# A new order of the attention step, queries turned in pairs, and a first expert choice over eight batches

## The reference, cut to what matters

```
x = x + tanh(g_xattn[0]) * conv_mix(layernorm(x), k, bias, ctx, ctx)        # stage A
x = x + tanh(g_ffn[0])   * moe(layernorm(x))        # stage B: shared FFN + top 2 of 8 experts
x = x + tanh(g_xattn[1]) * mha(layernorm(x), ctx, ctx)  # stage C: 16 heads, causal
x = x + tanh(g_ffn[1])   * lora_moe(layernorm(x))   # stage D: one FFN, top 2 of 8 adapters
```

## Time and profile before

| what | us |
|---|---|
| median of 3 runs (lowest to highest) | 826.37 (821.41 to 831.22) |
| the profiled execution: time, and span of the trace | 828.8, 827.1 |
| PE busy | 699.6 (85%) |
| DVE busy | 577.7 (70%) |
| ACT busy | 306.2 (37%) |
| POOL busy | 233.1 (28%) |
| granted TensorE clock over the span | 0.928 |

### The profile page before, as it was taken

How to read it: one execution, slowest core, us unless ns; L and a number is a source line. 1 busy time by engine, 2 the same in 40 slices (tenths; PEclk the granted TensorE clock), 3 DMA queues, 4 the chain that set the end, 5 groups by cost and what they waited for, 6 DMA issues and landing times.

```text
span 827.1 us, 12725 instructions
## 1 busy us (share of the span) xinstructions
PE 699.6 (85%) x4214; PEld 564.3 (68%) x4214; DVE 577.7 (70%) x1229; ACT 306.2 (37%) x539; POOL 233.1 (28%) x246
## 2 busy tenths in 40 slices
PE   2788899678989499999698798987698999999994
PEld 1555668467877499988465465555577888888883
DVE  5888887747476267763767878784378778768664
ACT  2201101036443144432356575754244345243331
POOL 1988797650027300005676111111000000000000
PEclk9999999979999699999679998966799999999996
DMA  8202100034204344424654122100101001011000
GB/s 292 77 13 71 38 13 14 1 99 125 85 27 145 104 118 123 119 71 83 122 80 89 58 67 72 52 1 1 51 1 52 1 27 51 1 33 45 26 0 26
DMA packets 42920, 51.22 MB, mean 62 GB/s; under 512 B 7088, under 2 KB 36976, under 8 KB 42224
## 3 DMA queue, kind: packets, MB, share of 16 engines
q1 hardware_dynamic: 36720, 41.98, 16.3%
q0 software_dynamic: 6144, 8.52, 5.1%
HBM read 36.88 MB, written 13.59 MB: 61 GB/s over the span
## 4 chain that ended last, share of the span: by engine, by line
PE 49%; DVE 16%; ACT 6%; issue 5%; POOL 3%; DMA 2%; DVEq 0%; ACTq 0%; SPq 0%
PE bank L2173 22%; PE bank L2023 5%; PE bank L2043 4%; PE bank L1959 4%; POOL x_d L644 3%; PE bank L2094 3%; PE bank L2080 2%; DVE A L1518 2%; DVE small L1508 2%; ACT A L891 2%; PE bank L2105 1%; PE bank L1973 1%; DVE A L1066 1%; DMA A<-rows_d 1%; PE bank L2011 1%
## 5 line engine op out<-in xcount | busy, mean ns | idle before, releaser
L2173 PE MATMUL bank<-R 128*128 128x512 f32 (+3 forms) x1080 | 221.6, 366 | 21.5 <-DVE R L1632 6.3
L2173 PEld LDWEIGHTS bank<-R 128*128 128x128 f32 (+1 forms) x1080 | 183.4, 193 | 56.9 <-issue 7.4
L650 POOL DMA_INDIRECT X<-y_d,A x32 | 50.3, 1571 | 119.0 <-DMA y_d<-A 101.8
L1959 PE MATMUL bank<-R 128*128 128x512 f32 x264 | 66.7, 404 | 5.3 <-DVE R L1389 4.3
L1867 PE MATMUL bank<-A 128*128 128x256 f32 x128 | 42.6, 415 | 23.3 <-issue 11.3
L600 POOL TENSOR_TENSOR A<-A 128x256 f32<-128x256 f32 x64 | 58.8, 919 | 12.4 <-DVE A L1156 12.3
L1959 PEld LDWEIGHTS bank<-R 128*128 128x128 f32 x264 | 50.0, 195 | 15.5 <-issue 4.4
L1508 DVE TENSOR_REDUCE small<-bank 128x8 f32<-128x1024 f32 x32 | 39.1, 1220 | 28.2 <-PE bank L2084 28.2
L702 POOL TENSOR_TENSOR A<-A 128x512 f32<-128x512 f32 x4 | 5.1, 1286 | 179.3 <-DVE A L1626 179.3
L1156 DVE TENSOR_TENSOR A<-bank,A 128x512 f32<-128x512 f32 x64 | 43.7, 683 | 15.7 <-PE bank L1869 12.5
L1145 DVE TENSOR_TENSOR A<-A 128x512 f32<-128x512 f32 x64 | 52.5, 822 | 2.1 <-ACT A L728 2.1
(11 more groups left out here) (272 smaller groups left out, 1346.9 us busy)
## 6 DMA issues: line engine op xcount, KB each, us to landing
A<-x_d SPq DMA_DIRECT2D x39, 132.0 KB, 2.1
y_d<-A SPq DMA_DIRECT2D x39, 128.0 KB, 1.7
A<-rows_d SPq DMA_DIRECT2D x4, 1024.0 KB, 4.8
A<-in_w SPq DMA_DIRECT2D x8, 480.0 KB, 3.6
A<-in_w SPq DMA_DIRECT2D x5, 512.0 KB, 3.7
A<-in_ctx_one SPq DMA_DIRECT2D x8, 272.0 KB, 3.6
A<-in_ctx_half SPq DMA_DIRECT2D x8, 256.0 KB, 2.7
A<-in_ctx_nat SPq DMA_DIRECT2D x4, 512.0 KB, 3.7
```

The costliest lines, as they stand in the source:

```text
L650: nc.gpsimd.indirect_dma_start(out=X[:, b], out_offset=None, in_=y_d[:, :], in_offset=bass.IndirectOffsetOnAxis(ap=y_slots[:, b, r:r + 1], ...
L1959: mm = nc.tensor.matmul(dst, wX[:, a0:a0 + P], mX[:, k], start=(m == 0), stop=(m == 5))
L2173: mm = nc.tensor.matmul(dst, a, m, start=start and n == 0, stop=stop and n == len(prods) - 1, skip_group_check=skip)
```

## The change

- **Expert choice.** `PARTS` has two parts of eight batches, where it had four and twelve. The steps of `part_route(0)` leave the last heads of stage A and stand in stage B beside tiles 6 to 8 (8, 4, 8, 4 and 4 steps); `b_rank(0)` follows tile 8. ACT's exponential of the part moves to tile 7. POOL's 32 scatters become 16 and 16. What the first group still needs early, the sigmoid that scales its shared FFN, is made by a one-column path (`sg0`) at the end of stage A.
- **Early halves of x.** `b_high_x(0)` stands ahead of ACT's wait for `a_done`, and `b_low_x(0)` ahead of `a_finish(3)` on DVE.
- **Attention step.** On PE `c_turn_p(k+1)` goes from second to last place of the step. On ACT `c_take_ot` is first, then `c_evac`, the query copy, `c_exp`. PE's loop over groups is written out.
- **Queries.** Only queries 0 and 1 of group 0 are normed and turned ahead of the attention, and their norm and turn stand ahead of tile 23's `b_hidden` and `b_down`; the norm of queries 2 and 3 follows the first `c_shift`. Later queries are turned in steps 1, 3, 5 and 7 (all four of the last group in steps 4 to 7 of the group before).

```diff
-        PARTS = ((0, BG, small), (BG, B, A1[:, 13312:14304]))
+        PARTS = ((0, 2 * BG, A1[:, 3536:4048]), (2 * BG, B, A1[:, 13312:13824]))
...
+def q_turned_in(g, k):
+
+    if k in (1, 3) and g < G - 1:
+        return g, 2 + k // 2
+    if g < G - 2 and k in (5, 7):
+        return g + 1, k // 2 - 2
+    if g == G - 2 and k in TURN_AT:
+        return g + 1, TURN_AT.index(k)
+    return None
...
@@ ACT @@
+                if n in (7, 9):
+                    b_exp(n // 2 - 3)
...
-            b_exp(0)
+            act.wait_ge(expin_ready, 1)
+            nc.scalar.activation(sg0, sg0, ACT.Exp).then_inc(exp_ready, 1)
+            b_high_x(0)
             act.wait_ge(a_done, 1 + 2 * G)
-            b_high_x(0)
             b_silu_of(0)
...
@@ DVE, b_side and b_group @@
                 if n in (7, 8):
                     logits_copy(n - 5)
+                if 6 <= n < 9:
+                    choice.take(8)
...
                     b_hidden(n)
+                    if 7 <= n < 9:
+                        choice.take(4)
...
+                    if n == SJ * G - 2:
+                        rows_complete(0, 0, 2)
+                        c_norm(0, 2).take_all()
...
@@ DVE, main @@
             a_heads(G - 1, False)
+            b_low_x(0)
             a_finish(G - 1)
-            b_low_x(0)
+            logits_copy(0)
...
             c_shift(0, 0)
+            rows_complete(0, 2, 4)
+            c_norm(2, 4).take_all()
             c_shift(0, 1)
...
@@ PE, c_steps @@
-                    if k and (k < 6 or more):
-                        c_scores(g + (k + 2) // 8, (k + 2) % 8)
-                    if more and k in TURN_AT:
+                    turned = q_turned_in(g, k)
+                    if turned:
                         pe.wait_ge(ot_taken, 8 * g + k)
-                        c_turn_q(g + 1, TURN_AT.index(k))
+                        c_turn_q(*turned)
...
-                    if k < 7 or more:
-                        c_turn_p(g + (k + 1) // 8, (k + 1) % 8)
+                    if k and (k < 6 or more):
+                        c_scores(g + (k + 2) // 8, (k + 2) % 8)
                     if k:
                         c_turn_o(g, k - 1)
...
                     c_values(g, k)
+                    if k < 7 or more:
+                        c_turn_p(g + (k + 1) // 8, (k + 1) % 8)
```

More of the change, by code:

```diff
@@ L653, in gather @@
                     compute_op=ALU.add).then_inc(gathered[r][b % BG], 16)
[L655 to L660, removed]
+            for p, (lo, hi, _) in enumerate(PARTS):
+                pool.wait_ge(slots_ready, p + 1)
+                for b in range(lo, hi):
+                    scatter(b)
             def zero_keys():
@@ L950, in c_steps @@
                         d_norm_one(0, k - 2)
-            act.wait_ge(qT_turned, BG)
+                    if not more and k + 1 in TURN_AT:
+                        d_take_x0(TURN_AT.index(k + 1))
+                    if k < 6 or more:
+                        c_exp(g + (k + 2) // 8, (k + 2) % 8)
+                    if more and q_normed_in(g, k):
+                        gn, b = q_normed_in(g, k)
+                        if gn:
+                            act.wait_ge(qT_turned, BG * (gn - 1) + b + 1)
+                        c_norm_one(gn, b)
+                    if k in (1, 5):
+                        c_high(g, k // 4)
+            act.wait_ge(qT_turned, 2)
             act.wait_ge(h_ready, 1 + SJ * G)
-            for b in range(BG):
+            for b in range(2):
                 nc.scalar.activation(qT[:, b], bank[2][:, b * D:(b + 1) * D].rearrange("p (k t) -> p k t", k=DT),
@@ L1199, in a_heads @@
                         link(nc.vector.tensor_scalar(eoff, ramp[:], -float(CAP), float(E * CAP), ALU.mult, ALU.add))
-                        logits_copy(0)
-                    beside = norm if norm.left() else route if h > 8 else Steps()
-                    beside.take(1 if more else 2)
+                        dve.wait_ge(logits_ready, 1)
+                        nc.vector.tensor_scalar(sg0, TP[:, 0:BG * NR].rearrange("p (b e) -> p b e", b=BG)[:, :, E],
+                                                -1.0, None, ALU.mult).then_inc(expin_ready, 1)
+                    norm.take(1 if more else 2)
                     if h + 2 < NH0:
@@ L1216, in a_heads @@
                         a_skip(g + 1)
-                route.take_all()
                 norm.take_all()
+                if not more:
+                    dve.wait_ge(exp_ready, 1)
+                    link(nc.vector.tensor_scalar(sg0, sg0, 1.0, None, ALU.add))
+                    link(nc.vector.reciprocal(sg0, sg0))
+                    step.mark(nc.vector.tensor_scalar(sg[:, 0:BG], sg0, gate[:, 2:3], None, ALU.mult))
             N_TOPS = 11
@@ L1300, in route_step @@
                     elif i == 23:
[L1301 to L1302 removed]
+                        weight = rcp[:, 0:n].unsqueeze(2).to_broadcast([P, n, E])
+                        for rows, at, m in ((rows0, 0, BG), (rows1[:, 0:BG], BG, BG)) if p == 0 else (
+                                (rows1[:, BG:], 0, n),):
+                            step.mark(nc.vector.tensor_tensor(rows[:, :, D:], l2[:, at:at + m],
+                                                              weight[:, at:at + m], ALU.mult))
                     elif i == 24:
@@ L1555, in c_steps @@
                     norm.take((3, 3, 8, 8)[k % 4] if more and g == 0 else 3 if more else 6)
-                    if more and k == 3:
+                    if more and k == (2 if g == G - 2 else 3):
                         norm.take_all()
@@ L2335, in _ @@
                 b_group(g)
-                b_down(SJ * g + SJ - 1)
-            for b in range(BG):
+                if g + 1 < G:
+                    b_down(SJ * g + SJ - 1)
+            for b in range(2):
                 pe.wait_ge(vN_ready, BG * 2 * G + b + 1)
@@ L2349, in _ @@
             pe.wait_ge(ot_zeroed, 1)
-            with pe.Fori(0, G - 1) as g:
+            for g in range(G - 1):
                 c_steps(g, True)
```

65 lines of the change are left out of this document (30 added, 35 removed).

## The result

The changed kernel takes 819.23 us (median of 12 runs, 815.51 to 823.51), the kernel before 827.67 in the same comparison (12 runs, 821.41 to 833.6): a ratio of 0.9895, interval 0.9871 to 0.9918, or 8.7 us. The prediction said 806 and 796 to 817. The direction was right, the size was not: 819.2 is above the range, and 13 us of the forecast 21.6 did not come.

A forecast was written before the change was run, and what follows sets the result against it. No engine was taken as full: chains of waits between engines bound four places. Gains of 10.2 + 3.7 + 0 + 7.7 = 21.6 us gave 804.8 against the median, 806 with part of a low-clock restart; range 796 to 817.

The forecast's parts named there:

- the 3.7 us of the tiles, the scatters and the first block: End of stage B: 32 scatters follow the later choice, first block at 275.5 instead of 279.2, a gain of 3.7 us.
- the 7.7 us of the attention's order: Attention from 463.45 on: turn placed last saves half of DVE's 12.4 + 3.0 us of waits, 7.7 us.
- End of stage A and early halves: End of stage A into stage B: faster heads and earlier gate_up bring the first down product 10.2 us sooner.
- Choice in the tiles: Stage B, tiles 6 to 8: choice steps on DVE make PE late by about 1.5 us, the rank adds some 0.5.
- The wait before the first block: Between last tile and first block: PE's wait of 10.06 us behind the scatters shrinks to about 3.
- the rival of slower scatters: Before the first block: scatters slow to 1.6 us apart, costing 6.4, total 812.4; chance 0.12, shared with late halves.
- DVE ends the tiles at 270.85, so no more than 6.9: First block: DVE's end of the tiles, 272.4 with the delay, limits the gain there to 6.9 us.
- The keys' wait: Group 1's step 4, scores at 463.45: the keys' transfer holds PE, whose wait grows from 1.5 to 8.5 us.
- gate doesn't bind, 797.5: Rival at the scores at 463.45: they move with PE, giving 8.5 us more, total 797.5; chance 0.10.
- the rival with 0.20: Attention: the new order gives nothing because DVE's own list sets the pace, total 813.7; chance 0.20.
- part of one restart: Attention behind the keys: a low-clock restart step takes 7.18 us, 2.4 back; part of it was counted.
- a gate_up at 172: Start of stage B: if the early halves wait for something else, 6.4 us are given back, total 812.

The follow-up runs named there:

- after_small_again: The changed kernel with POOL's low halves of stage D's weights made for 8 of 960 columns only, timed again: ratio 0.9773 to the kernel before.
- high_later: The changed kernel with ACT's first high half of the weights in each group made in step 4 instead of step 1: ratio 0.9788 to the kernel before.
- the small cut: POOL's low halves of stage D's weights made for 8 of 960 columns only: ratio 0.9801 on the kernel before, 0.9719 on the changed kernel.

## Why the prediction was wrong

Two terms of the sum failed: the 3.7 us of the tiles, the scatters and the first block, where 1.6 were lost instead, and the 7.7 us of the attention's order, of which 0.6 came.

- **End of stage A and early halves: right.** 10.2 forecast, 11.2 measured, with the 1.28 of the table load where it was put. Heads came at 1.57 instead of 1.73, and `a_sum` at a mixed clock, 5.33 instead of 6.66. The activation follows 0.01 after the table load. So the drain that the Trainium skill, "ScalarE: Activation LUTs", section "What ACT_TABLE_LOAD costs", adds to the load does not show here either.
- **Choice in the tiles: nearly right.** 2.0 lost forecast, 2.9 measured. PE's wait at the turn in tile 7 grew from 0.52 to 1.42, by 0.9 where 1.5 was worked out; another 1.6 went ahead of the choice, at 192 us, where PE's down and gate_up products took 2.45 and 3.74 in place of 1.70 and 2.91, at a granted clock of 0.72 in place of 1.00.
- **The wait before the first block: wrong.** About 3 us forecast, 8.68 measured. The cadence and the place of the scatters were right, and the rival of slower scatters fell (1.42 apart). The step that failed is the bound "DVE ends the tiles at 270.85, so no more than 6.9": it takes the engines to be free when their counted work ends. PE and DVE each load 39 registers from then on, about 8.6 us on PE, and SP's 9.25 end only at 264.92. Before, this lay under the scatters' wait of 10.06, and only 1.4 us of that wait could be had. The code of before could have told it, since it has the loads between the last tile and the first block. Its trace shows them nowhere, but has room for them, in PE's 10.06 and in DVE's idle time there:

```profile
280.39 0.79 DVE L1464 TENSOR_TENSOR R<-bank,R 128x256 fp32r<-128x256 f32 x2 [9.54 <-ACT R L840]
```

- **The keys' wait: the place was right, its price was not.** The scores of group 1's step 4 came 8.7 earlier where the blocks came 9.6 earlier, though PE stood 13.2 ahead at the first scores. But there was no 8 us wait: the hit of 4.45, a wait of 2.00 for the values and the low clock brought PE there just in time, 0.33 before, so of its lead of 13.2 only 7.5 was left when it came to the gate. And the rival "gate doesn't bind, 797.5" fell with it: with the gate open the runs gained 0.6 to 2.6 us, not 8.5.
- **The attention's order: wrong, by most of its size.** 7.7 forecast, 0.6 measured behind the keys' wait (102.97 to 102.37, first scores behind it to last values). Taking half of DVE's 15.4 us of waits assumed that values and turn back need nothing that is late. The turn back needs the bank that DVE's `c_finish` reads, and DVE does that behind the shift and the norm steps. So a wait of PE for ACT became a wait for DVE: 6.2 us with the hits, 2.9 and 2.0 in the traces of after_small_again and high_later. The sum also put POOL's hits at nothing, and of the clock it took back only part of one restart, though idle time that goes came back as 2.3 to 4.2 us of longer products even without hits. This was the rival with 0.20, though not quite in its words: DVE is not the bound by its sum, but late at one place, and made later by the hits.

Here the Trainium skill spoke where I did not listen. "SBUF — State Buffer", section "Who interferes with whom", which the prediction cites for the scatters, also says that a DVE instruction with two inputs in SBUF contends with a GpSimd instruction that reads SBUF. The traces agree: the adds and norm steps above were hit, while the shift beside them, which reads a bank, kept its 1.22. That sentence does not cover the steps with one input that were hit.

The sum closes: 11.2 - 1.6 (tiles and block) - 0.9 (to the keys) + 0.6 (attention) + 0.9 (stage D, unexplained and within the spread of profiled runs) = 10.2. Against the forecast 21.6 it lacks 11.4: 7.1 in the attention and 5.3 in the tiles and the first block, with 1.0 more at the end of stage A. Two small slips decided nothing: a gate_up at 172 would give back 172 - 165.2 = 6.8, not 6.4, and 0.94 less 0.06 is 0.88, not 0.87.

## What to carry to other kernels

And when an order is changed to hide one wait, read what each moved instruction itself waits for, and look at the clock before counting idle time that goes as time gained.

## What the runs showed of the hardware

Loading 39 table entries into registers took PE about 8.6 us and SP 9.25, some 0.22 to 0.24 each. One at a time within the blocks it was nearly hidden: from the first to the last down product of the blocks 89.36 and 89.19 us passed, where it was 89.04. DVE instructions with operands in SBUF alone, with one input or two, stood until POOL's was done, through two POOL instructions in a row (4.45 us in place of 0.42); the granted clock from 440 to 455 us, at the end of that one and behind it, was 0.68. PE's stretch behind the keys' wait, with the small cut, had 5.6 us less idle time and 4.2 us more busy time at 0.91 than at 0.95.
